# A two-layer decoder on one core: eight biases of a score tile on GpSimd, and the order of several stages changed

## The reference

```
x = x + L0_attn(ln(x))    # 16 heads of 16, 4 kv heads, over (seq 4, batch 256): each token attends to its 4-long axis
x = x + L0_xattn(ln(x))   # per batch, softmax of q^T k over the first feature axis
x = x + L0_ffn(ln(x))     # ternary weights, activations rounded to 8 bits by row maxima, gelu
x = x + L1_attn(ln(x))    # low-rank q and kv (64), causal, 16 heads
x = x + L1_xattn(ln(x))   # all 1,024 queries against all 1,024 context tokens, 16 heads; q, k, v, probabilities rounded
x = x + L1_moe(ln(x))     # softmax router, top 8 of 64 (32 experts, 32 empty ones), capacity 128, silu
```

## Time and profile before

| | us |
|---|---|
| median of 3 runs (lowest, highest) | 594.05 (591.17, 597.64) |
| the profiled execution | 593.47 |
| its span, first to last instruction | 591.7 |
| busy PE, DVE, ACT, POOL | 449.2, 448.7, 323.3, 232.8 |
| mean granted TensorE clock | 0.941 |

### The profile page before, as it was taken

One profiled execution on the slowest core, in us unless ns is written; L12 is line 12 of the kernel. 1 busy time (PEld: TensorE's weight loads), 2 busy tenths in 40 slices (PEclk: granted clock), 3 DMA queues, 4 the chain that ended last, 5 costly groups with the idle time before them and its releaser, 6 DMA issues.

```text
span 591.7 us, 10719 instructions
## 1 busy us (share of the span) xinstructions
PE 449.2 (76%) x3774; PEld 285.1 (48%) x3774; DVE 448.7 (76%) x968; ACT 323.3 (55%) x606; POOL 232.8 (39%) x304
## 2 busy tenths in 40 slices
PE   2998846678887886877777787787775879888871
PEld 1535522445565654344444445453434348667660
DVE  5899698989699569999898989889998643322135
ACT  1424524445793654888788788778882105333330
POOL 7543210015584554033332414243110167888740
PEclk9999987999999899799898989989997979999997
DMA  8760000000025002799999999999997199895545
GB/s 294 201 227 1 0 1 2 1 0 2 1 53 91 3 1 37 124 178 173 162 182 157 177 169 175 166 177 162 187 186 189 29 323 287 228 214 88 89 75 184
DMA packets 186101, 73.89 MB, mean 125 GB/s; under 512 B 159105, under 2 KB 183617, under 8 KB 186049
## 3 DMA queue, kind: packets, MB, share of 16 engines
q1 hardware_dynamic: 181056, 65.35, 52.5%
q0 software_dynamic: 4992, 7.87, 7.3%
HBM read 27.56 MB, written 7.88 MB: 60 GB/s over the span
## 4 chain that ended last, share of the span: by engine, by line
DVE 43%; PE 26%; issue 11%; DMA 7%; ACT 6%; POOL 5%; SPq 1%; POOLq 0%; DVEq 0%; ACTq 0%
DVE nm L1666 22%; DVE AT L1489 5%; DMA sums<-A,slot_token 4%; PE ps L878 3%; PE ps L1067 3%; PE ps L895 3%; POOL A L625 2%; POOL sums L635 2%; PE ps L1079 2%; DVE b L1672 2%; PE ps L861 2%; PE ps L1140 2%; PE ps L896 1%; PE ps L953 1%; PE ps L969 1%
## 5 line engine op out<-in xcount | busy, mean ns | idle before, releaser
L819 ACT ACTIVATE A<-ps,b,sq 128x1024 int16<-128x1024 f32 x128 | 154.0, 1203 | 40.0 <-DVE b L1672 35.2
L1666 DVE TENSOR_REDUCE nm<-ps 128x1 f32<-128x1024 f32 x128 | 154.9, 1210 | 8.8 <-PE ps L1140 8.8
L1140 PE MATMUL ps<-big,ctx_sb 128*128 128x512 bf16 x256 | 81.9, 403 | 45.7 <-ACT A L819 42.6
L1150 PEld LDWEIGHTS ps<-VI,A 128*128 128x128 f16 x1024 | 43.3, 97 | 41.1 <-DMA A<-A 15.6
L1140 PEld LDWEIGHTS ps<-big,ctx_sb 128*128 128x128 bf16 x256 | 18.9, 101 | 73.2 <-ACT A L819 54.3
L1736 DVE TENSOR_TENSOR AT<-AT,ps 128x128 f32<-128x128 f32 x32 | 9.1, 286 | 57.6 <-ACT AT L835 36.9
L1150 PE MATMUL ps<-VI,A 128*128 128x16 f16 x1024 | 45.1, 170 | 5.4 <-DMA A<-A 4.9
L635 POOL DMA_INDIRECT sums<-A,slot_token x24 | 39.4, 1640 | 12.3 <-ACT A L845 6.2
L625 POOL DMA_INDIRECT A<-x_rows,slot_token x32 | 35.1, 1098 | 22.6 <-DVE big L1660 13.1
L845 ACT ACTIVATE A<-ps,A 128x256 f32<-128x256 f32 x32 | 15.1, 473 | 40.7 <-DMA sums<-A,slot_token 37.2
L1258 PE MATMUL ps<-A 128*128 128x128 f32 x256 | 35.8, 284 | 1.7 <-DMA A<-in 0.4
(11 more groups left out here) (304 smaller groups left out, 1047.2 us busy)
## 6 DMA issues: line engine op xcount, KB each, us to landing
A<-in SPq DMA_DIRECT2D x32, 256.0 KB
A<-in SPq DMA_DIRECT2D x32, 128.0 KB
A<-in SPq DMA_DIRECT2D x2, 1024.0 KB, 14.3
sums<-zeros SPq DMA_DIRECT2D x4, 512.0 KB, 4.7
A<-A SPq DMA_TRANSPOSE x128, 3.3
A<-sums SPq DMA_DIRECT2D x8, 256.0 KB, 4.5
X<-in SPq DMA_DIRECT2D x1, 1024.0 KB, 6.1
big<-in SPq DMA_DIRECT2D x1, 1024.0 KB, 8.8
```

The source lines that it names most:

```text
L819: a.activation(Y5[:, n % YB, :], ps[:, 2 * (n % 3):2 * (n % 3) + 2, :], ACT.Exp, scale=sq5[:, q, h:h + 1], bias=b5[:, n % 4:n % 4 + 1], ac ...
L1140: done = T.matmul(ps[:, 2 * (n % 3) + c, :], QT5[:, q % 2, h // 2, h % 2, :], KT5[:, h // 2, c * 512:(c + 1) * 512], start=True, stop=True)
L1150: done = T.matmul(ps[:, 6 + q % 2, h * HD:(h + 1) * HD], PT5h[:, m % YB, k, :], VI[:, k, h * HD:(h + 1) * HD], start=(k == 0), stop=(k == 7))
L1666: v.tensor_reduce(nm5[:, n % 4:n % 4 + 1], ps[:, 2 * (n % 3):2 * (n % 3) + 2, :].rearrange("p a c -> p (a c)"), AX.X, ALU.max, negate=True ...
```

## The change

The diff has 731 lines. In stage 5, at eight positions of each tile's sixteen, POOL computes the bias in place of DVE, with a semaphore of its own; POOL's list is written unit by unit so that its other work stands at fixed positions among these. The score banks rotate by one. Its core (constants, POOL's new functions and loop, then DVE's part; `pad_queries` and `quantise_queries` hold the padding and the quantising of before, the first behind a wait for POOL's own bias n):

```diff
+        PBIAS_AT = (0, 1, 2, 4, 6, 11, 14, 15)
+        PBIAS = [n for n in range(U5) if n >= LAG5 and (n - LAG5) % H in PBIAS_AT]
+        def wait_bias(eng, n):
+            if n in PBIAS:
+                eng.wait_ge(S["pbias5_ready"], PBIAS.index(n) + 1)
+            else:
+                eng.wait_ge(S["bias5_ready"], n + 1 - sum(m <= n for m in PBIAS))
...
+            def score_bias(n):
+                h, q = n % H, n // H
+                pool.wait_ge(S["max5_ready"], n + 1)
+                if n >= 4:
+                    pool.wait_ge(S["exp5_ready"], n - 3)
+                g.tensor_scalar(b5[:, n % 4:n % 4 + 1], nm5[:, n % 4:n % 4 + 1], sq5[:, q, h:h + 1], LN255, ALU.mult, ALU.add).then_inc(S["pbias5_ready"], 1)
...
+            for n in range(LAG5, U5 + LAG5 + H):
+                q, at = (n - LAG5) // H, (n - LAG5) % H
+                ahead = q + 2 < NT
+                if n in PBIAS:
+                    score_bias(n)
+                if at == WO_H and ahead:
+                    ln_rstd("q", q + 2, q + 3)
+                    ln_apply("q", q + 2)
+                if at == WP_H:
+                    if 1 <= q < NT - 1:
+                        pad_queries(q + 1, n)
+                    if q >= 1:
+                        ln_rstd("r", q - 1, q)
+                    if 1 <= q < NT:
+                        ln_apply("r", q - 1)
+                    if ahead:
+                        add_bp(q + 2)
+                if at == Q5_H + 1 and ahead:
+                    quantise_queries(q + 2)
...
+                    if n - 4 in PBIAS:
+                        wait_bias(dve, n - 4)
-                    v.tensor_reduce(nm5[:, n % 4:n % 4 + 1], ps[:, 2 * (n % 3):2 * (n % 3) + 2, :].rearrange("p a c -> p (a c)"), AX.X, ALU.max, negate=True).then_inc(S["max5_ready"], 1)
+                    v.tensor_reduce(nm5[:, n % 4:n % 4 + 1], ps[:, 2 * ((n + 1) % 3):2 * ((n + 1) % 3) + 2, :].rearrange("p a c -> p (a c)"), AX.X, ALU.max, negate=True).then_inc(S["max5_ready"], 1)
+                    if n not in PBIAS:
...
```

In the front, the ternary passes move between the copies of the key/value tiles, the first transpose stands among the projections, key/value tiles 6 and 7 go behind the cross-attention (into banks 6 and 7), and POOL's clearing is placed anew (PE, ACT and POOL, in this order):

```diff
             for t in range(NT - 2):
                 project_kv(t)
-            keep_warm(7, 8)
+                if t == 3:
+                    to_T(1, 0, AT[:, 0, :], S["prod0_ready"], 9)
...
-            for t in range(NT - 2, NT):
-                project_kv(t)
...
+            for t in range(NT - 2, NT):
+                project_kv(t)
...
             for t in range(NT - 2):
                 copy_kv(t)
+                if t == 3:
+                    copy_T(1, 0, 0)
+                if t in (3, 4):
+                    act.wait_ge(S["wscale_ready"], 2)
+                    a.activation(w_flat[t - 3], w_flat[t - 3], ACT.Identity, scale=wrec[:, t - 3:t - 2], bias=roundc[:, 0:1]).then_inc(S["wq_step"], 1)
...
-            a.activation(VABS[:, :, :], KV[:, :, D:2 * D], ACT.Abs).then_inc(S["vabs_ready"], 1)
+            a.activation(VABS[:, 0:NT - 2, :], KV[:, 0:NT - 2, D:2 * D], ACT.Abs).then_inc(S["vabs_ready"], 1)
+            for t in range(NT - 2, NT):
+                copy_kv(t)
+            act.wait_ge(S["kv_copied"], NT)
+            a.activation(VABS[:, NT - 2:NT, :], KV[:, NT - 2:NT, D:2 * D], ACT.Abs).then_inc(S["vabs_ready"], 1)
...
+            score_products(pool, g, 1, S["prod1_ready"], range(0, 1))
             g.memset(zeros[:, :], 0.0).then_inc(S["pads_ready"], 1)
+            score_products(pool, g, 1, S["prod1_ready"], range(1, 2))
             g.memset(kpart[:, :, :, 3, :].rearrange("p t h d -> p (t h) d"), 0.0).then_inc(S["pads_ready"], 1)
-            score_products(pool, g, 1, S["prod1_ready"], range(0, 3))
+            score_products(pool, g, 1, S["prod1_ready"], range(2, 3))
...
-            norm_rstd(1)
-            pool.wait_ge(S["w_ternary"], 2)
             g.memset(V4[:, :, :, HD:HD + 1], 1.0).then_inc(S["pads_ready"], 1)
             g.memset(V4[:, :, :, HD + 1:2 * HD], 0.0).then_inc(S["pads_ready"], 1)
+            norm_rstd(1, 0, 1)
             pool.wait_ge(S["tp_psum"], 2 * NT)
             g.memset(MM4[:, :, :], 0.0).then_inc(S["pads_ready"], 1)
+            norm_rstd(1, 1, 2)
```

More of the change, by code:

```diff
@@ L440, in _ @@
             store_rows(NT - 2)
+            for e in range(4, 12):
+                sp.wait_ge(wg_loaded[e % 4], 32 * (e // 4))
+                load_weights(e)
             store_rows(NT - 1)
@@ L1022, in _ @@
                 T.matmul(ps[:, bank + 1, :], wupk[LOW:P, g, :, :].rearrange("p r c -> p (r c)"), CNT[LOW:P, cols], start=True, stop=True).then_inc(S["upk_psum"], 1)
+                if 2 <= j < 6:
+                    values4(2 * j - 4)
+                    values4(2 * j - 3)
+                if j == 6:
+                    pe.wait_ge(S["v4_ready"], NT - 1)
+                    pe.wait_ge(S["vscale_ready"], 4)
+                    for a in range(2):
+                        for k in range(KD):
+                            last = T.matmul(ps[:, 0, (a * KD + k) * P:(a * KD + k + 1) * P], svb[:, a * KD + k, :], identf[:, :], start=True, stop=True)
+                    last.then_inc(S["vstat_psum"], 1)
             def heads4(buf, g, b, lo, hi):
@@ L1048, in _ @@
                 for t in range(2):
-                    last = T.transpose(ps[:, b, t * P:(t + 1) * P], MM4[:, 2 * b + t, :], identf[:, :])
+                    last = T.transpose(ps[:, b % 2, m4_cols(b) + t * P:m4_cols(b) + (t + 1) * P], MM4[:, 2 * b + t, :], identf[:, :])
                 last.then_inc(S["m4T_psum"], 1)
+                if b >= NB - 2:
+                    keep_warm(2, 3)
             def out_proj(t, bank, lo):
@@ L1265, in _ @@
                     T.matmul(ps[:, 2, 0:D], HE[:, e % 2, :], WD[:, e % WS, :], start=True, stop=True).then_inc(S["ye_psum"], 1)
+                if s in (NE, NE + 1):
+                    assert COMBINE[s - NE + 4] == s - 4
+                    for c in range(4):
+                        combine(s - NE + 4, c)
                 for n in range(2, NE // EG):
@@ L1270, in _ @@
                         list_spread(n)
-            for i, e in enumerate(COMBINE):
-                for c in range(min(4, max(0, NE + 2 - e - 4)), 4):
+            for i in (6, 7):
+                for c in range(4):
                     combine(i, c)
@@ L1292, in norm_stats, with norm @@
                     v.bn_aggr(mv[:, order[s - 1], :], stats[:, order[s - 1], :]).then_inc(S["aggr_ready"], 1)
-            def norm(n):
+            def norm(n, lo=0, hi=NT):
                 order = PARITY_ORDER if n == 1 else IN_ORDER
-                for s in range(NT):
+                for s in range(lo, hi):
                     t = order[s]
@@ L1399, in _ @@
-            dve.wait_ge(S["dq3_step"], 3)
-            v.tensor_scalar(qs3[:, :], qs3[:, :], 127.0, None, ALU.mult).then_inc(S["dq3_step"], 1)
-            dve.wait_ge(S["dq3_step"], 5)
-            for s in range(NT + 1):
-                if s < NT:
-                    v.tensor_scalar(XN[:, s, :], XN[:, s, :], qs3[:, s:s + 1], ROUND, ALU.mult, ALU.add).then_inc(S["qx_step"], 1)
-                if s >= 1:
-                    dve.wait_ge(S["qx_step"], s)
-                    v.tensor_scalar(QX[:, s - 1, :], XN[:, s - 1, :], -ROUND, None, ALU.add).then_inc(S["qx_ready"], 1)
+            for half in range(2):
+                tiles = slice(4 * half, 4 * half + 4)
+                norm(2, 4 * half, 4 * half + 4)
+                dve.wait_ge(S["xn_ready"], 2 * NT + 4 * half + 4)
+                v.tensor_reduce(am3[:, tiles], XN[:, tiles, :], AX.X, ALU.max, apply_absolute_value=True).then_inc(S["dq3_step"], 1)
+                dve.wait_ge(S["dq3_step"], 4 * half + 1)
+                v.tensor_scalar(am3[:, tiles], am3[:, tiles], EPS, 1.0 / 127, ALU.max, ALU.mult).then_inc(S["dq3_step"], 1)
+                dve.wait_ge(S["dq3_step"], 4 * half + 2)
+                v.reciprocal(qs3[:, tiles], am3[:, tiles]).then_inc(S["dq3_step"], 1)
+                v.tensor_scalar(dq3[:, tiles], am3[:, tiles], wmean[:, 0:1], None, ALU.mult).then_inc(S["dq3_step"], 1)
+                dve.wait_ge(S["dq3_step"], 4 * half + 4)
+                for s in range(4 * half, 4 * half + 5):
+                    if s < 4 * half + 4:
+                        v.tensor_scalar(XN[:, s, :], XN[:, s, :], qs3[:, s:s + 1], ROUND, ALU.mult, ALU.add).then_inc(S["qx_step"], 1)
+                    if s >= 4 * half + 1:
+                        dve.wait_ge(S["qx_step"], s)
+                        v.tensor_scalar(QX[:, s - 1, :], XN[:, s - 1, :], -ROUND, None, ALU.add).then_inc(S["qx_ready"], 1)
```

226 lines of the change are left out of this document (98 added, 128 removed).

## The result

The changed kernel takes 576.75 us (median of 4 runs, 574.87 to 582.68) against 592.96 for the kernel before on the same chip: a ratio of 0.973, interval 0.968 to 0.978. Beside it in a later session it took 577.28 (5 runs) against 593.81, ratio 0.975 (0.972 to 0.977). The forecast was 578, between 568 and 589. The profiled execution took 575.69, its span 574.0: 17.7 less than before.

What follows compares the result with a forecast made beforehand. Stage 5 was taken as bound by VectorE without slack, passing side work on to ScalarE, the rest as a chain of short stages. Nine terms summed to -15.8 us, from median 594.05 to 578, range 568 to 589.

Steps and rivals of the forecast that it cites:

- Stage 5: Eight biases a tile moved from VectorE to GpSimd gain 1.0 us a tile over six tiles: -6, ends -2 and -9.
- the slower rival: Stage 5: GpSimd's queue gives ScalarE two biases late, 3.4 us a tile lost; kernel 606; chance 0.06.
- The sign I gave: Stage 5's tile at 26.3 us in place of 27.3, ScalarE's wait for both kinds of bias well under 35.2.
- The zeroing: GpSimd's `kpart` clearing beside VectorE's first three products slows them: +1.1 us, from 0 to +1.9.
- First projection: Earlier ternary passes and first transpose, no warming matmuls; PE's idle 1.73 goes: -1.2 us, ends -1.7 and +0.8.
- Cross-attention: Key/value tiles 6 and 7 placed after it let scores and exponential start earlier: -3.8 us, ends -2.3 and -4.8.
- Low-rank: Transposes and value products leave PE's chain ahead of the up-projections: -0.9 us, ends 0 and -2.3.
- Self-attention: Batch maxima in two banks and matmuls warming the clock speed first score products: -1.0 us, ends 0 and -2.2.
- FFN, router: FFN row scales in two halves: -1.2 us; six router instructions off the path to the last tile's output: -1.3.
- Experts: Weights 4 to 11 loaded ahead of the router cut GpSimd's idle before its first scatter-add: -1.5 us, ends 0 and -2.4.
- The rival that stage 5 gives nothing: Transposes' DMA share, or hops and three score buffers, eat the gain; other terms leave 584 us; chance 0.17.
- The rival that the front gives little: Zeroing costs 1.9, cross-attention gives 2.3, FFN, low-rank and clock nothing: 1.6 us instead of 7.0, so 583; chance 0.12.

Runs made afterwards that it cites:

- late loads: Changed kernel with weights of experts 4 to 11 loaded behind the router again: first gather to first scatter-add 15.3 us, against 12.0 with early loads.
- old list: Changed kernel with the old list of experts whose results PE sums, and its old loop: 576.26 us (one run).

## Why the prediction was right, and where it was not

- *Stage 5.* The mechanism was right and the size too small: 7 to 8.6 in place of 6. The step that failed is the reading that ScalarE, too, needs 1.38 a unit. It needs 1.19, so once VectorE leads, ScalarE catches up by 0.19 a unit, which I had not counted. The hop was taken as 0.08 and is 0.13, which four times a tile is 0.2 more: it did not matter. That GpSimd's queue would hold is borne out: the longest wait for its bias is 0.9, and 1.4 at most in the other kernels with eight. Twelve biases show the price of the slower rival: 30.5 - 27.2 = 3.3 a tile more than before. That this is close to its 3.4 is chance: the rival reckoned with two late biases, 2.2 and 1.2, and it was one, 4.3 late behind position 6's work.
- *The sign I gave.* A tile at 26.3 came as 25.0 to 26.6. But ScalarE's waits "well under 35.2" did not: they are 34.9. The view of waits, from which the prediction started, showed the right cause and was no measure of the gain.
- *The zeroing.* +1.1 was the wrong choice between the ends; it is 0 to 0.3. The row I took as nearest had the same operation on VectorE, but what its neighbour did, reading or only writing, decided. What I had not counted, though the earlier trace rows show it, is that the old V4 clearing held VectorE in the cross-attention: the 0.9 that its old place costs.
- *First projection.* -1.2 became +0.7: the idle 1.73 went, but the first transpose among the key/value tiles opened 1.24 of idle in front of the last two of them, and these then ran at half clock. That step counted the early transpose as free. Where the half clock ended early, in five kernels, the stretch came out 0.9 to 1.1 shorter than before, near the forecast. What the eight removed warming matmuls are worth no run shows by itself.
- *Cross-attention.* -3.8 became -3.0. The scores could start when forecast, but after 3.4 of idle they were cold for a part: 5.18 for 3.72. That is 1.5 lost, more than the shortfall; the clearing's 0.9 made up for part.
- *Low-rank.* -0.9 became +1.3. This step did count removed warming matmuls as free: 1.8 lost by the clock, against 0.5 from the placing.
- *Self-attention.* -1.0 became -2.1; all of it is the clock, as the step said. I took 1.0 of the 1.6 that three slow groups make; the six matmuls are worth 2.6.
- *FFN, router.* -1.1 and -1.3, as forecast, the first by luck: it is so only where the loop's first tiles are warm, and in five of twelve kernels the stretch was 2.4 longer than before.
- *Experts.* -1.5 became -4.0, beyond the step's own end of -2.4. Its cause is right (the loads). That further scatter-adds gain nothing is less sure: 80.0 became 77.7 from first to last, but the changed kernels lie between 77.4 and 79.1 whatever their edit, late loads (78.6) and old list (77.9) among them. What is left to 80.0, 0.9 to 2.6, neither edit explains, and before the change there is one profile.
- *The ends.* The poor ends add up to -2.4, so 591.6 and not the 590 of the prediction; the range it gave, to 589, does not hang on it.

The rival that stage 5 gives nothing is excluded by its 8.6 and by the run with the biases back on VectorE; the slower one by GpSimd's waits. The rival that the front gives little came nearest: the stretches up to stage 5 gave 3.8 in place of 7.0, where it had 1.6.

## What to carry to other kernels

When two engines show the same period, only one of them sets it: look for a place where the other runs unhindered before calling both full. Work handed to an engine with an in-order queue costs its own few tenths only as long as no long job stands in front; place it by what lies ahead of it, and take no more of it than covers the other engine's side work (four of sixteen did nearly as well as eight here). Matmuls that look useless are part of a timing: before taking them out, or after opening a gap on PE, count the stretch behind it at half clock. And where identical instructions take different times from run to run, one profile of an edit proves little: compare the stage over several.

## What the runs showed of the hardware

- PE's clock fell to the 1.2 GHz level after single idle stretches of 1.24 and 3.43 us, and after a row of gaps of 0.3 to 0.9. The length of the slow stretch differed from one execution to another of the same PE instructions: in the key/value tiles it ended between 42 and 57 us, and the same first exponential started between 63.6 and 69.3. An idle of 1.47 before the same transposes was followed by a clock of 0.53 in one kernel and of 1.00 in another, and 1.73 before the first projection by 1.00.
- A two-column VectorE instruction beside a GpSimd MEMSET of 1.75 took 1.37 in place of 0.17, and 1.12 in the earlier trace rows, each to the MEMSET's end; three two-input products beside a MEMSET of 1.81 lost nothing.
